# Score products of two attention heads in the two halves of the partitions, values in pieces, and edits at the start and at the transition to the experts

## The reference

```
xn = layernorm(x)
s  = attention(xn)          # 16 heads of 16, causal: softmax(q k^T / 4 + bias) v, then w_out
g  = silu(swiglu_ffn(xn))   # 768 hidden, int weights / 127
x  = x + s * g
xn = layernorm(x)
s  = hyena(xn)              # short convolution, then a long one by rfft / irfft
g  = silu(experts(xn))      # top 2 of 20 experts for each of 4096 rows
x  = x + s * g
```

## Time and profile before

| | us |
|---|---|
| median of 3 runs (lowest, highest) | 1087.86 (1086.83, 1089.52) |
| the profiled execution | 1087.2 |
| its span | 1085.5 |
| PE busy in the span | 961.2 (89%) |
| DVE busy | 718.7 (66%) |
| ACT busy | 479.2 (44%) |
| POOL busy | 344.0 (32%) |

### The profile page before, as it was taken

One profiled execution on the slowest core, in us unless ns is written; L12 is line 12 of the kernel. 1 busy time (PEld: TensorE's weight loads), 2 busy tenths in 40 slices (PEclk: granted clock), 3 DMA queues, 4 the chain that ended last, 5 costly groups with the idle time before them and its releaser, 6 DMA issues. The chain is left out here.

```text
span 1085.5 us, 19164 instructions
## 1 busy us (share of the span) xinstructions
PE 961.2 (89%) x5936; PEld 731.6 (67%) x5936; DVE 718.7 (66%) x1459; ACT 479.2 (44%) x887; POOL 344.0 (32%) x610
## 2 busy tenths in 40 slices
PE   1889999999999999999999989855899989999995
PEld 1665776776776676676676766644666778888884
DVE  7555476576576576576676465464375339999997
ACT  1434445445545545545545534532222334444441
POOL 6203313613613613623623532352000054333310
PEclk9978999999999999999999996987899989999998
DMA  5864854644543534534534530095566653334321
GB/s 175 159 155 62 154 179 62 116 157 62 113 151 68 114 144 74 111 143 78 94 138 82 100 113 2 18 342 214 175 209 209 200 170 123 125 119 122 122 66 39
DMA packets 87596, 137.23 MB, mean 126 GB/s; under 512 B 9907, under 2 KB 63347, under 8 KB 85364
## 3 DMA queue, kind: packets, MB, share of 16 engines
q1 hardware_dynamic: 69188, 101.40, 38.0%
q0 software_dynamic: 6144, 16.79, 5.2%
q10 hardware_dynamic: 12208, 18.35, 4.9%
HBM read 79.88 MB, written 55.57 MB: 125 GB/s over the span
## 5 line engine op out<-in xcount | busy, mean ns | idle before, releaser
L1461 DVE TENSOR_REDUCE Mneg<-PS 128x2 f32<-128x1024 f32 (+2 forms) x192 | 194.3, 1043 | 95.3 <-PE PS L968 95.3
L1222 ACT ACTIVATE PT<-PS 128x512 f32<-128x512 f32 (+1 forms) x384 | 169.3, 538 | 146.7 <-PE PS L992 146.3
L992 PE MATMUL PS<-qs,ks 96*128 96x512 f32 (+3 forms) x512 | 133.6, 370 | 13.7 <-DMA qs<-mrow 6.9
L1714 POOL TENSOR_TENSOR idle_p<-neghalf 128x1 f32<-128x1 f32 x128 | 25.2, 197 | 335.0 <-ACT PT L1222 335.0
L964 PE MATMUL PS<-ks,qs 96*128 96x256 f32 (+3 forms) x512 | 121.1, 346 | 3.0 <-issue 2.1
L992 PEld LDWEIGHTS PS<-qs,ks 96*128 96x128 f32 x512 | 89.5, 195 | 44.5 <-ACT PT L1222 27.7
L788 PE MATMUL PS<-xnT,Wgu 128*128 128x512 f32 x384 | 102.9, 409 | 4.3 <-ACT V L1167 2.4
L1887 PE MATMUL PS<-Wes,xbT 128*128 x336 | 98.4, 402 | 3.5 <-issue 2.1
L1720 POOL TENSOR_SCALAR_AFFINE_SELECT PT<-PT 128x256 f32<-128x256 f32 x256 | 100.2, 415 | 0.0
L964 PEld LDWEIGHTS PS<-ks,qs 96*128 96x128 f32 x512 | 78.6, 199 | 13.0 <-issue 10.0
L788 PEld LDWEIGHTS PS<-xnT,Wgu 128*128 128x128 f32 x384 | 69.6, 190 | 23.5 <-DVE h L1404 3.5
(11 more groups left out here) (227 smaller groups left out, 1710.7 us busy)
## 6 DMA issues: line engine op xcount, KB each, us to landing
qs<-qk_parts SPq DMA_DIRECT2D x96, 128.0 KB
ks<-qk_parts SPq DMA_DIRECT2D x96, 128.0 KB
xb<-slots_in SPq DMA_DIRECT2D x84, 128.0 KB, 2.3
slots_out<-yb ACTq DMA_DIRECT2D x28, 384.0 KB, 3.2
qk_parts<-qhl SPq DMA_DIRECT2D x16, 512.0 KB, 2.8
qk_parts<-khl SPq DMA_DIRECT2D x16, 512.0 KB, 3.1
xn2T_parts<-xn2T SPq DMA_DIRECT2D x8, 1024.0 KB, 4.8
xT<-xn2T_parts ACTq DMA_DIRECT2D x7, 1024.0 KB
```

The costliest lines, as they stand in the source:

```text
L992: last = pe.matmul(PS[:, 4 + n, col:col + T - P * kt], ks[:, hd, P * kt:P * kt + P], qs[:, hd, P * kt:T], start=True, stop=True)
L1222: act.activation(PT[:, g % 2, j, 512 * n:512 * n + width], PS[:, 4 + n, 0:width], ACT.Exp, scale=SCALE).then_inc(S["exped"], 1)
L1461: dve.tensor_reduce(out=Mneg[:, 0, qt, heads[0]:heads[-1] + 1], in_=all_of, op=ALU.max, axis=AX.X, negate=True).then_inc(S["maxed"], 1)
```

## The change

- **Layout.** `qs` and `ks` become 128 partitions by 8 pairs: head 2a lies in partitions 0 to 63, head 2a+1 in 64 to 127. Score products contract over 48 rows of a half (`KU`), transposed scores over 50 (`KT`), where rows 48 and 49 hold the maxima and the ones. Neighbouring heads of a unit write to different banks; the unit of 128 keys, formerly in one bank, takes two, and its mask is two matmuls of 256 columns rather than one of 512.
- **DMAs.** Each block of a group goes by two DMAs, one for each half: 12 a group rather than 7, of half the size, and none of zeros. The rows of maxima go by two DMAs; `m_in` rises by 32 a group, and the first transposed head waits for both.
- **Order on PE.** The transposed heads stand after the units 1, 3, 4, 5 (before: 1, 2, 4, 5). In steps 2 to 4 the values are made in pieces: key tiles 0 and 1 at u = 1, tile 2 at u = 5, tile 3 at u = 6, ahead of the maxima's rows. In step 5 they stay whole.
- **ACT.** `OT` of group s−3 is taken at the head of step s, ahead of the exponentials; the last at the end of step 5.
- **Start.** The clears of `qs` and `ks` go. POOL sets the upper 32 rows of each half of `ks` to one in two memsets of 4096 columns, behind the reciprocal roots and the memset of `V`; SP's first stack waits for both.
- **Transition.** `Inv`'s low part (POOL) moves behind the sends, into the experts' stretch, where DVE's first use waits for it. ACT runs an idle Gelu ahead of `split_x1`. The experts' block 1 is loaded by ACT, and SP reads the row numbers of blocks 0 and 2 ahead of its wait for the sends.

```diff
@@ layout, units
-                return [PS[:, slot + n // 2, 256 * (n % 2):256 * (n % 2) + 256] for n in range(4)], both
...
+            both = PS[:, slot:slot + 2, 0:2 * keys].rearrange("p a (b k) -> p a b k", b=2)
+            return [PS[:, slot + n % 2, keys * (n // 2):keys * (n // 2) + keys] for n in range(4)], both
...
+            return slice(HR * (hd % 2), HR * (hd % 2) + rows), hd // 2
...
-                        pe.matmul(out, qs[:, hd, P * qt:P * qt + P], ks[:, hd, 0:keys], start=n % a_bank == 0,
+                        rows, pair = half_of(GH * g + j, KU)
+                        pe.matmul(out, qs[rows, pair, P * qt:P * qt + P], ks[rows, pair, 0:keys], start=n < 2,
...
-                            last = pe.matmul(PS[:, 4 + n, col:col + T - P * kt], ks[:, hd, P * kt:P * kt + P],
-                                             qs[:, hd, P * kt:T], start=True, stop=True)
+                            last = pe.matmul(PS[:, 4 + n, col:col + T - P * kt], ks[rows, pair, P * kt:P * kt + P],
+                                             qs[rows, pair, P * kt:T], start=True, stop=True)
@@ DMAs
-                    sp.dma_start(f(qs[M0:M0 + 2, GH * g:GH * g + GH, :]), mrow[:, :]).then_inc(S["m_in"], 16)
+                    for q in range(2):
+                        sp.dma_start(f(qs[HR * q + M0:HR * q + M0 + 2, 2 * g:2 * g + 2, :]),
+                                     mrow[GH * NT * q:GH * NT * (q + 1), :]).then_inc(S["m_in"], 16)
@@ order on PE
+                TURNED_AT = (1, 3, 4, 5)
+                VALUES_AT = {1: (0, 1), 5: (2,)}
...
-                            if u == 1 and 2 <= s:
-                                values(b, s - 2)
+                            if s == NG + 1 and u == 1:
+                                values(b, s - 2, range(NT))
+                            elif 2 <= s <= NG and u in VALUES_AT:
+                                values(b, s - 2, VALUES_AT[u])
...
+                            if 2 <= s <= NG and u == NU - 1:
+                                values(b, s - 2, (3,))
@@ ACT
+                        if s >= 3:
+                            keep_heads(b, s - 3)
...
-                            if j == 1 and s >= 2:
-                                keep_heads(b, s - 2)
+                        if s == NG + 1:
+                            keep_heads(b, NG - 1)
@@ start
-                clear_queries(0)
-                clear_queries(1)
...
-                for g in range(NG):
-                    pool.memset(f(ks[M0:M0 + 2, GH * g:GH * g + GH, :]), 1.0).then_inc(k_set, 1)
-                pool.wait_ge(k_set, NG)
+                for q in range(2):
+                    pool.memset(f(ks[HR * q + HR // 2:HR * q + HR, :, :]), 1.0).then_inc(k_set, 1)
+                pool.wait_ge(k_set, 2)
@@ transition
-                pool.wait_ge(t_hi, 3)
-                pool.tensor_tensor(Inv[:, LO, :, :], st_i[:, :, :], f(Inv[:, HI, :, :]), ALU.subtract)
```

More of the change, by code:

```diff
@@ L981, in transposed_scores @@
                     hd = GH * g + j
+                    rows, pair = half_of(hd, KT)
                     if hd == 0:
@@ L1006, in values @@
                                              PT[:, g % 2, j, COL[kt]:COL[kt] + T - P * kt],
-                                             start=kt == 0, stop=kt == NT - 1)
-                    last.then_inc(S["pv"], 1)
+                                             start=kt == 0, stop=kt == NT - 1, skip_group_check=True)
+                    if NT - 1 in tiles:
+                        last.then_inc(S["pv"], 1)
                 SPECTRUM = {(NG, 1): (0, 0), (NG, 2): (0, 1), (NG, 4): (1, 0), (NG + 1, 0): (1, 1)}
@@ L1460, in maxima @@
                     _, all_of = scores_of_unit(slot, u)
-                    dve.tensor_reduce(out=Mneg[:, 0, qt, heads[0]:heads[-1] + 1], in_=all_of, op=ALU.max, axis=AX.X,
-                                      negate=True).then_inc(S["maxed"], 1)
+                    made = Mneg[:, 0, qt, heads[0]:heads[-1] + 1]
+                    if keys <= 256:
+                        made = made.rearrange("p (b a) -> p a b", a=2)
+                    dve.tensor_reduce(out=made, in_=all_of, op=ALU.max, axis=AX.X, negate=True).then_inc(S["maxed"], 1)
                 def parts_of_maxima(b, g):
@@ L1835, in half_rows, with row_of_block, load_block @@
             return ap.rearrange("(j k p) d -> j p k d", p=P, k=HALF)[n]
-        def load_block(sp, block, after=0):
-            row = sp.value_load(block_row[0:1, block:block + 1], min_val=0, max_val=NROWS - P)
+        def row_of_block(eng, block):
+            return eng.value_load(block_row[0:1, block:block + 1], min_val=0, max_val=NROWS - P)
+        def load_block(sp, block, row, after=0):
             at_least(sp, transposed, after)
@@ L1853, in _ @@
             def _(sp):
+                first_rows = {n: row_of_block(sp, n) for n in (0, 2)}
                 sp.wait_ge(S["sent"], 128 * B)
                 for n in range(NBLK):
-                    load_block(sp, n, after=n - AHEAD + 1)
+                    if n == 1:
+                        continue
+                    row = first_rows[n] if n in first_rows else row_of_block(sp, n)
+                    load_block(sp, n, row, after=n - AHEAD + 1)
                     if n == AHEAD:
@@ L1918, in store, with before, _ @@
                                   ).then_inc(yb_out[h_ % 2], 16)
-                in_turns(act, lambda: None, turn)
+                def before():
+                    row = row_of_block(act, 1)
+                    act.wait_ge(S["sent"], 128 * B)
+                    load_block(act, 1, row)
+                in_turns(act, before, turn)
                 store(NBLK - 1)
+            @block.gpsimd
+            def _(pool):
+                pool.tensor_tensor(Inv[:, LO, :, :], st_i[:, :, :], f(Inv[:, HI, :, :]), ALU.subtract
+                                   ).then_inc(t_lo, 1)
             @block.vector
```

99 lines of the change are left out of this document (46 added, 53 removed).

## The result

The changed kernel takes 1143.4 us (four runs, 1140.7 to 1149.3) where the kernel before takes 1088.7: ratio 1.051, 95% interval 1.046 to 1.056. The forecast was 1061, with a range from 1046 to 1102. It was wrong in sign and size, and the first rival, the granted clock, is where the time went.

What follows compares the result with a forecast made beforehand. PE, busy 89% of the span, was taken to bound the kernel, with attention steps a PE/DVE loop and the transition a chain: 1087.2 − 19 − 2.5 − 5 = 1060.7, plus 0.7 for the median: 1061 us, range 1046 to 1102.

Steps and rivals of the forecast that it cites:

- rival 1: Granted clock falls in steps 1 and 2 of six middle sequences: +37 us, 1098; with step 3, 1118; chance 0.32.
- The price of a change of form: About a dozen changes of array form in an attention group: 0.03 us each, 0.4 a step, range 0 to 0.1 each.
- the pairs' gain: Score products of two heads side by side: 1.07 us a group, 1.0 after the extra mask matmul; range −0.07 to 1.8.
- rival 2: Changes of form cost 0.1 us or more, pairs are paid back: 1080, or 1088 at 0.15 a change; chance 0.12.
- The body of a sequence: All attention terms of one sequence together: −2.4 us; for eight sequences −19, range −40 to +10.
- Step 2: Attention step of 10.46 us, a loop over PE and DVE: 9.75 forecast, gain 0.7, range 0.1 to 1.1.
- Step 3: Attention step booked like step 2: gain 0.7, range 0.1 to 1.1; the two such steps together −1.4 us.
- Step 1: Attention step without values; head 0 to 0.6 us later, DVE's wait goes, pairs give some: −0.2, range −0.6 to +0.6.
- The rest with group 0: Group 0's units between projections: −0.6 us (−0.9 to +0.3); step 4, without units: −0.2 (−0.4 to +0.3).
- The second DMA: For the maxima's rows, ahead of the first transposed head: adds at most 0.65 us or so, at least nothing.
- Start and transition: Less contest between POOL and DVE: start −2.5 us (−1 to −8), transition −5 (−3 to −7).
- the first of my two cases: At the start, `xn` needs a gap between POOL's instructions for each of four, ending near 17.9, 1.7 us earlier.

Runs made afterwards that it cites:

- narrow: Kernel before with score products over 48 rows and transposed scores over 50 (96 before), no heads side by side, one DMA of maxima, old order: ratio 1.120, 1247.9 us.
- layout_only: Changed kernel with the order of the kernel before; layout, DMAs, start and transition left: ratio 1.064 to the kernel before.
- folded: Changed kernel with the mask matmuls also over 64 rows of a half: ratio 0.985 to the kernel before, 1089 us.
- order_only: Kernel before with the new order alone, 96 rows, one DMA of maxima, no pairs: ratio 0.983.
- two_dmas: Kernel before with the rows of maxima written by two DMAs of one row each: ratio 1.000.
- folded_order: Changed kernel with masks over 64 rows and the new order only in steps 1 and 2, no added matmuls: ratio 1.001 to the kernel before.
- folded_best: Changed kernel with masks over 64 rows, new order only in steps 1 and 2, four full matmuls in step 1's wait: ratio 0.985 to the kernel before.
- folded_filled: Changed kernel with masks over 64 rows and four full matmuls in step 1's wait for the maxima: ratio 0.981 to the kernel before, 1089 us.

## Why the prediction was wrong

- **The choice between forecast and rival 1 failed.** The forecast took the middle sequences at the full clock. I gave rival 1 0.32, because the wait for the maxima would stay short of the 2.07 us behind which the clock had fallen, and one of 0.62 had done nothing. The wait did stay short, 0.69, shorter even than the 1 to 1.5 that rival 1 had given as one of its reasons. But it was the wrong row to decide by: `narrow` has no such wait, and its clock falls with PE busy. The middle sequences ran at PEclk 0.83 and lost 63.0 us, more than the whole loss. The share of busy time, which I read in the earlier trace rows, does not tell how much of the array works. That the packed layout lets the clock fall is shown (`layout_only`), and so is the part of the changes of form in it (`folded`); whether the missing rows have a part of their own is open.
- **The price of rival 1** was 37 us for two low steps in each of six sequences. A low step 2 was set at 3.3 us by a step of the first sequence in which the clock had come back before its end (PEclk 0.74, the row below). Low all through, step 2 took 16.54 rather than 9.82 us, 6.7 more. And the clock was low for about a third of the middle sequences, in steps 1 to 3 and once more after them, not for two steps.

```profile
82.89:96.68 13.79, 13.08 (x78) 7.34 (x78) 7.06 (x10) 6.17 (x15) 3.63 (x12) 0.74 0.42 61
```

- **The price of a change of form** was set at 0.03 us by a row after a 64-row product with only 20 columns. Measured: 0.06 to 0.09, within the range that I kept. With about twelve a group it eats the pairs' gain, which for a unit of 512 columns was sized rightly: 0.20 against 0.21. The Trainium skill, "TensorEngine Tiling (Array Packing)", Key Properties, says that a change of tiling mode drains TensorE. The prices in `narrow` (0.09) and `folded` (0.06) agree with that rule. So rival 2 was true in its mechanism as well, beside rival 1, and I had given it 0.12.
- **The body of a sequence**, booked at −2.4 us, gave about −0.4 at full clock. Step 2 came out at 9.82, forecast 9.75, but by luck: with the new order and no pairs at all it is 9.66 (`order_only`), so what I had booked for the pairs there was not what brought it. Step 3, booked at the same −0.7, became 11.01, 0.2 longer than before: it has gate products at its end and DVE's waits are hidden there, so PE is the limit (10.82 busy of 10.82 before) and only PE's own work counts. Step 1: 10.81 with four matmuls added and PEclk 0.94, forecast 11.0. The rest with group 0: +0.4, forecast −0.8.
- **The second DMA** costs nothing (`two_dmas`), within the stated range.
- **Start and transition**: first transposes at 17.14 rather than 19.76, −2.6 (−2.5 forecast). Of that 1.7 is the shorter stretch of `xn` (9.39 rather than 11.07), the first of my two cases; the other 0.95 is `rstd`, which starts earlier (6.51 rather than 7.46) and was in no term. `rstd` to first block is −5.1 (−5 forecast), but 3.2 and 2.1 us more pass before and behind it, so that the stretch from the last turning to the end is as long as before.

## What to carry to other kernels

Fewer rows and more changes of form can cost the clock even where PE stays busy: read what part of the array a busy PE uses and how often that changes, and price the clock before the columns. If heads are packed into halves, bring the matmuls between them, such as a mask, into the same form; that took a loss of 4 to 6% away and left between nothing (`folded_order`) and a gain of 1.5% (`folded`). Then compare with the plain layout under the same order and edits: here the packed one was not ahead of it. And a PE-bound step gains only what PE itself does less, so sum each step by its own limit and don't carry one step's waits to the next.

## What the runs showed of the hardware that I had not expected

- PE busy without a pause and still 2.4 GHz lost: in `narrow` the clock fell to 1.2 GHz in the row at 578.63 us with no idle time of PE behind 574.01. Once low, it stayed through busy stretches (step 2 of the changed kernel: 16.54 of 16.54 us busy at PEclk 0.50).
- Four full matmuls of 512 columns in a wait of each sequence are worth 1.6% of the kernel in one pair of runs (`folded_best` beside `folded_order`), and nothing clear in another (`folded_filled` beside `folded`, 0.981 and 0.985). Ten were no better than four, on another chip.
- A change between 64 and 128 rows costs 0.09 us in a unit whose columns are the same.
- The kernel before takes 1088 to 1118 us on different chips, with a mean granted clock from 0.96 down to 0.94. Why one chip holds it better than another stays open, as does how much the changes of form and how much the missing rows each weigh in its fall.
